# Mixture-of-experts dispatch on one core: the first expert's columns made first, 16-bit tables with the chunk innermost, a semaphore per first gathered tile

## What is computed

```python
probs = softmax(xn @ router_w.T + router_b)          # 4096 x 8
gates, idx = top_k(probs.T, cap)                     # cap = 4096/8 = 512 tokens for each expert
xe = xn[idx]
hmid = gelu(einsum('ech,efh->ecf', xe, fc1_w) + fc1_b)      # 256 -> 1024
ye = einsum('ecf,ehf->ech', hmid, fc2_w) + fc2_b            # 1024 -> 256
out = zeros.at[idx].add(ye * gates)
out = out / max(sum of the gates of a token, 1e-9)
```

## Time and profile before

| | |
|---|---|
| runs | 1294.95, 1296.77, 1298.42 us; median 1296.77 |
| the profiled execution's own time | 1302.38 us |
| its span | 1300.7 us |
| mean granted TensorE clock | 0.91 |
| busy share: PE, DVE, ACT, POOL | 88%, 80%, 59%, 31% |
| instructions: PE, DVE, ACT, POOL | 8470, 2233, 929, 397 |
| self-attention and cross-attention | about 0 to 1000 us |
| routing and dispatch, PE nearly idle | about 1000 to 1067 us |
| eight experts | about 1067 to 1300 us |

### The profile page before, as it was taken

How to read it: one execution, slowest core, us unless ns; L and a number is a source line. 1 busy time by engine, 2 the same in 40 slices (tenths; PEclk the granted TensorE clock), 3 DMA queues, 4 the chain that set the end, 5 groups by cost and what they waited for, 6 DMA issues and landing times. The chain is left out here.

```text
span 1300.7 us, 24570 instructions
## 1 busy us (share of the span) xinstructions
PE 1138.8 (88%) x8470; PEld 625.0 (48%) x8470; DVE 1046.4 (80%) x2233; ACT 763.1 (59%) x929; POOL 399.1 (31%) x397
## 2 busy tenths in 40 slices
PE   5888799999999999899999999988874049999994
PEld 3555443333333333333333333357763038889984
DVE  6988799899999999899999999427775975666651
ACT  2333127788787888688887878843453004556561
POOL 5777861212021211121121000022100032665663
PEclk9988769999999999899999999989785557999997
DMA  3567565542244413431343000045422021454432
GB/s 107 169 221 230 202 121 164 107 97 49 46 83 79 73 38 67 80 73 35 68 84 76 19 15 16 19 117 205 148 69 86 0 65 49 129 157 105 113 97 25
DMA packets 84103, 120.38 MB, mean 93 GB/s; under 512 B 23248, under 2 KB 57040, under 8 KB 82960
## 3 DMA queue, kind: packets, MB, share of 16 engines
q1 hardware_dynamic: 64832, 75.84, 18.9%
q0 software_dynamic: 15984, 39.86, 16.4%
q10 hardware_dynamic: 3168, 3.15, 0.8%
HBM read 75.67 MB, written 42.21 MB: 91 GB/s over the span
## 5 line engine op out<-in xcount | busy, mean ns | idle before, releaser
L696 DVE TENSOR_REDUCE b_max_halves<-banks 128x1 f32<-128x512 f32 x1024 | 628.8, 681 | 27.1 <-PE banks L763 26.8
L638 ACT ACTIVATE b_probs<-banks 128x1024 f32<-128x1024 f32 x512 | 519.9, 1025 | 143.0 <-PE banks L815 141.3
L763 PE MATMUL banks<-b_k,b_q 62*128 62x512 f32 x1024 | 400.5, 473 | 3.8 <-DVE b_max L713 2.1
L815 PE MATMUL banks<-b_q,b_k 64*128 64x512 f32 x1024 | 389.2, 458 | 11.5 <-DMA b_q<-b_max_rows 5.1
L785 PE MATMUL banks<-b_probs,b_v 128*32 128x256 f32 (+1 forms) x3840 | 321.9, 407 | 2.3 <-ACT b_out L625 0.3
L815 PEld LDWEIGHTS banks<-b_q,b_k 64*128 64x128 f32 x1024 | 161.1, 186 | 228.3 <-issue 154.4
L763 PEld LDWEIGHTS banks<-b_k,b_q 62*128 62x128 f32 x1024 | 166.5, 191 | 37.8 <-DVE b_max_halves L696 33.6
L785 PEld LDWEIGHTS banks<-b_probs,b_v 128*32 128x32 f32 x3840 | 76.0, 108 | 166.6 <-issue 86.8
L464 POOL TENSOR_TENSOR b_att<-b_out,b_rec_spread 128x512 f32<-128x512 f32 x32 | 41.1, 1284 | 309.0 <-DMA b_rec_spread<-reciprocals 308.8
L395 POOL DMA_DIRECT2D b_q<-q_stacks x60 | 31.7, 531 | 253.2 <-PE banks L785 233.4
L1693 DVE TENSOR_TENSOR e_hTl<-e_hT,e_hTh 128x512 fp32r<-128x512 f32 x64 | 44.5, 696 | 53.9 <-ACT e_hT L1453 53.9
(11 more groups left out here) (230 smaller groups left out, 1546.0 us busy)
## 6 DMA issues: line engine op xcount, KB each, us to landing
e_w<-in_w SPq DMA_DIRECT2D x16, 1024.0 KB
v_tiles<-a_v SPq DMA_DIRECT2D x8, 1024.0 KB, 9.1
q_stacks<-a_parts SPq DMA_DIRECT2D x32, 256.0 KB
k_stacks<-a_parts SPq DMA_DIRECT2D x32, 256.0 KB
b_q<-q_stacks POOLq DMA_DIRECT2D x30, 256.0 KB, 6.5
b_k<-k_stacks POOLq DMA_DIRECT2D x30, 256.0 KB, 7.2
b_v<-v_tiles POOLq DMA_DIRECT2D x15, 512.0 KB, 9.4
b_q<-b_max_rows SPq DMA_DIRECT2D x256, 2.0 KB
```

Of the source, the lines that this page charges most:

```text
L638: nc.scalar.activation(pr[:, S % NP, u], ps[:, 2 * u:2 * u + 2, :], ACT.Exp, scale=D ** -0.5).then_inc(s_ex[u], 1)
L696: v.tensor_reduce(mxp[:, (k // NB) % 2, s, p, t, kh:kh + 1], ps[:, bank(last), :], AX.X, ALU.max)\
L763: nc.tensor.matmul(ps[:, bank(last), :], qs[g][stack, p, at:at + P], ks[g][stack, p, CH * kh:CH * kh + CH], start=True, stop=True).then_in ...
L815: return nc.tensor.matmul(ps[:, 2 * u + s, :], ks[g][stack, u, P * kt:P * kt + P], qs[g][stack, u, CH * h:CH * h + CH], start=True, stop=True)
```

## The change

Six edits in `experts`:

1. **Layouts.** `hi`, `rv`, `w3` and `cmp_` have the chunk (or the block) innermost instead of the column. `tid`, the chunks' numbers, goes from 32 to 16 bits. The moving operand of a compaction now has its columns 32 elements of 16 bits apart.
2. **Two pieces.** The block tests and places are done for expert 0's 32 columns first (`first`), and for the 224 others (`others`) after expert 0's indicators.
3. **DVE's order.** `tokens(1)`, its indicators and `lower_w1` follow `first_slots(0)` in this order, the block tests of the others stand ahead of it; `rows(0)` stands ahead of `weights()`.
4. **Gathers of expert 0** count on a semaphore per tile, `s_g0[h]`; those of expert 2, 4 and 6 on `s_g[0]`, whose counts are 64 lower.
5. **Transposes.** `rows` on PE goes tile by tile (both halves of one tile, then the next), for every expert; for expert 0 it waits for each tile by itself.
6. **Expert 0's gate compaction** stands behind hidden unit 3 on PE, and so do `first_weights` and the tables of expert 2 on DVE.

```diff
-        hi = sb("d_hi", [P, 2, NTT, CT], BF16)
-        tid = sb("d_tid", [P, NTT])
+        hi = sb("d_hi", [P, 2, CT, NTT], BF16)
+        tid = sb("d_tid", [P, NTT], BF16)
-        w3 = sb("d_w3", [P, E * NTT, 3], BF16)
+        w3 = sb("d_w3", [P, 3, E * NTT], BF16)
-        rv = sb("d_rv", [P, 2, NTT, CT, NV], BF16)
+        rv = sb("d_rv", [P, 2, NV, CT, NTT], BF16)
-        cmp_ = sb("d_cmp", [P, 2, CT, NV])
+        cmp_ = sb("d_cmp", [P, 2, NV, CT])
+        s_g0 = [sem(f"e_first_tile{h}_gathered") for h in range(CT)]
...
                     g.indirect_dma_start(xe[:, x, h, :], None, xrow,
-                                         bass.IndirectOffsetOnAxis(ap=idx[:, n, h:h + 1], axis=0)).then_inc(s_g[x], 16)
+                                         bass.IndirectOffsetOnAxis(ap=idx[:, n, h:h + 1], axis=0))\
+                        .then_inc(s_g[x] if n else s_g0[h], 16)
...
-            for h in range(CT):
-                ins = v.tensor_scalar(ge[:, h, :], qf, P * h + 0.5, None, ALU.is_ge)
-            step(ins)
-            step(v.tensor_tensor(lo[:], ge[:, 1, :], ge[:, 2, :], ALU.add))
-            step(v.tensor_tensor(lo[:], lo[:], ge[:, 3, :], ALU.add))
-            step(v.scalar_tensor_tensor(lob[:], lo[:], -float(P), qf, ALU.mult, ALU.add))
+            def blocks(at):
+                for h in range(CT):
+                    ins = v.tensor_scalar(ge[:, h, at], qf[:, at], P * h + 0.5, None, ALU.is_ge)
+                step(ins)
+            def places(at):
+                step(v.tensor_tensor(lo[:, at], ge[:, 1, at], ge[:, 2, at], ALU.add))
+                step(v.tensor_tensor(lo[:, at], lo[:, at], ge[:, 3, at], ALU.add))
+                step(v.scalar_tensor_tensor(lob[:, at], lo[:, at], -float(P), qf[:, at], ALU.mult, ALU.add))
...
-                at = lambda h: ge[:, h:h + CT, chunks(n)].rearrange("p h k -> p k h")
+                at = lambda h: ge[:, h:h + CT, chunks(n)]
                 here(v.tensor_tensor(hi[:, x], at(0), at(1), ALU.subtract))
-                v.tensor_tensor(rv[:, x, :, :, 0], hi[:, x], tid[:].unsqueeze(2).to_broadcast([P, NTT, CT]), ALU.mult)
-                return v.tensor_scalar(rv[:, x, :, :, 1], hi[:, x], pid[:], None, ALU.mult)
+                v.tensor_tensor(rv[:, x, 0], hi[:, x], tid[:].unsqueeze(1).to_broadcast([P, CT, NTT]), ALU.mult)
+                return v.tensor_scalar(rv[:, x, 1], hi[:, x], pid[:], None, ALU.mult)
...
-            for n in range(2):
-                tokens(n, n)
-                if n == 1:
-                    first_slots(0)
-                    dve.wait_ge(s_w1h, 1)
-                    lower_w1()
-                for m in range(NTT // R):
-                    indicate(n, n, m)
+            first, others = slice(0, NTT), slice(NTT, E * NTT)
+            blocks(first)
+            places(first)
+            tokens(0, 0)
+            for m in range(NTT // R):
+                indicate(0, 0, m)
+            blocks(others)
+            first_slots(0)
+            places(others)
+            tokens(1, 1)
+            for m in range(NTT // R):
+                indicate(1, 1, m)
+            dve.wait_ge(s_w1h, 1)
+            lower_w1()
             first_slots(1)
+            rows(0)
             weights()
-            rows(0)
...
-                        if start and f == 1:
+                        if start and f == 3:
                             for m in range(2):
                                 first_weights(m)
...
-                    ins = mm(ps[:, 2, 0:CT * NV], oh[:, x, k // R, :, k % R], rv[:, x, k].rearrange("p h m -> p (h m)"),
+                    ins = mm(ps[:, 2, 0:CT * NV], oh[:, x, k // R, :, k % R], rv[:, x, :, :, k],
...
             def rows(i, x):
-                pe.wait_ge(s_g[x], 64 * i + 64)
-                for k in range(KC):
-                    for h in range(CT):
+                if not (isinstance(i, int) and i == 0 and x == 0):
+                    pe.wait_ge(s_g[x], 64 * i + (64 if x else 0))
+                for h in range(CT):
+                    if isinstance(i, int) and i == 0 and x == 0:
+                        pe.wait_ge(s_g0[h], 16)
+                    for k in range(KC):
...
-                        if start and f == 0:
+                        if start and f == 3:
                             pe.wait_ge(s_cc, 2)
                             pe.wait_ge(s_rvb, 1)
```

More of the change, by code:

```diff
@@ L1588, in tokens @@
                 here = Chain(dve, s_hi, n)
-                at = lambda h: ge[:, h:h + CT, chunks(n)].rearrange("p h k -> p k h")
+                at = lambda h: ge[:, h:h + CT, chunks(n)]
                 here(v.tensor_tensor(hi[:, x], at(0), at(1), ALU.subtract))
-                v.tensor_tensor(rv[:, x, :, :, 0], hi[:, x], tid[:].unsqueeze(2).to_broadcast([P, NTT, CT]), ALU.mult)
-                return v.tensor_scalar(rv[:, x, :, :, 1], hi[:, x], pid[:], None, ALU.mult)
+                v.tensor_tensor(rv[:, x, 0], hi[:, x], tid[:].unsqueeze(1).to_broadcast([P, CT, NTT]), ALU.mult)
+                return v.tensor_scalar(rv[:, x, 1], hi[:, x], pid[:], None, ALU.mult)
             def weigh(n, x):
-                return v.tensor_tensor(rv[:, x, :, :, 2:NV], hi[:, x].unsqueeze(3).to_broadcast([P, NTT, CT, 3]),
-                                       w3[:, chunks(n), :].unsqueeze(2).to_broadcast([P, NTT, CT, 3]), ALU.mult)
+                return v.tensor_tensor(rv[:, x, 2:NV], hi[:, x].unsqueeze(1).to_broadcast([P, 3, CT, NTT]),
+                                       w3[:, :, chunks(n)].unsqueeze(2).to_broadcast([P, 3, CT, NTT]), ALU.mult)
             def weights():
@@ L1610, in weights @@
                                      ALU.mult))
[L1611 to L1614, removed]
+                step(v.tensor_copy(w3[:, 0], wt[:]))
+                step(v.tensor_tensor(wr[:], wt[:], w3[:, 0], ALU.subtract))
+                step(v.tensor_copy(w3[:, 1], wr[:]))
+                step(v.tensor_tensor(w3[:, 2], wr[:], w3[:, 1], ALU.subtract))
                 for n in range(2):
@@ L1627, in first_slots @@
                 dve.wait_ge(s_cm, n + 1)
-                v.tensor_copy(cmp_[:, n, :, 0:2],
-                              ps[:, 2, 2 * P * n:2 * P * n + CT * NV].rearrange("p (h m) -> p h m", m=NV)[:, :, 0:2])\
+                v.tensor_copy(cmp_[:, n, 0:2],
+                              ps[:, 2, 2 * P * n:2 * P * n + 2 * CT].rearrange("p (m h) -> p m h", h=CT))\
                     .then_inc(s_cc, 1)
                 dve.wait_ge(s_cc, n + 1)
-                v.scalar_tensor_tensor(idx[:, n, :], cmp_[:, n, :, 0], float(P), cmp_[:, n, :, 1], ALU.mult, ALU.add)\
+                v.scalar_tensor_tensor(idx[:, n, :], cmp_[:, n, 0], float(P), cmp_[:, n, 1], ALU.mult, ALU.add)\
                     .then_inc(s_ix, 1)
@@ L1637, in first_weights @@
                 dve.wait_ge(s_cmb, 2)
-                v.tensor_copy(cmp_[:, n, :, 2:NV],
-                              ps[:, 2, 2 * P * n:2 * P * n + CT * NV].rearrange("p (h m) -> p h m", m=NV)[:, :, 2:NV])\
+                v.tensor_copy(cmp_[:, n, 2:NV],
+                              ps[:, 2, 2 * P * n + 2 * CT:2 * P * n + CT * NV].rearrange("p (m h) -> p m h", h=CT))\
                     .then_inc(s_ccb, 1)
                 dve.wait_ge(s_ccb, n + 1)
-                step(v.tensor_tensor(wx[:, n, :], cmp_[:, n, :, 2], cmp_[:, n, :, 3], ALU.add))
-                v.tensor_tensor(wx[:, n, :], wx[:, n, :], cmp_[:, n, :, 4], ALU.add).then_inc(s_wx, 1)
+                step(v.tensor_tensor(wx[:, n, :], cmp_[:, n, 2], cmp_[:, n, 3], ALU.add))
+                v.tensor_tensor(wx[:, n, :], wx[:, n, :], cmp_[:, n, 4], ALU.add).then_inc(s_wx, 1)
             def slots(n, x):
@@ L1648, in slots @@
                 dve.wait_ge(s_cm, n + 1)
-                v.tensor_copy(cmp_[:, x].rearrange("p h m -> p (h m)"), ps[:, 2, 0:CT * NV]).then_inc(s_cc, 1)
+                v.tensor_copy(cmp_[:, x].rearrange("p m h -> p (m h)"), ps[:, 2, 0:CT * NV]).then_inc(s_cc, 1)
                 dve.wait_ge(s_cc, n + 1)
                 loop = Chain(dve, s_dex, 2 * n - 4)
-                part = lambda m: cmp_[:, x:x + 1, :, m]
+                part = lambda m: cmp_[:, x:x + 1, m]
                 loop(v.scalar_tensor_tensor(idx[:, at, :], part(0), float(P), part(1), ALU.mult, ALU.add))
@@ L1765, in first_compact @@
             def first_compact(n, part, m, s):
-                o = ps[:, 2, 2 * P * n:2 * P * n + CT * NV].rearrange("p (h m) -> p h m", m=NV)
+                o = ps[:, 2, 2 * P * n:2 * P * n + CT * NV].rearrange("p (m h) -> p m h", h=CT)
                 for k in range(R * m, R * m + R):
-                    ins = mm(o[:, :, part], oh[:, n, k // R, :, k % R], rv[:, n, k, :, part], start=(k == 0), stop=(k == NTT - 1))
+                    ins = mm(o[:, part, :], oh[:, n, k // R, :, k % R], rv[:, n, part, :, k], start=(k == 0), stop=(k == NTT - 1))
                 if m == NTT // R - 1:
```

## The result

| | before | after |
|---|---|---|
| runs | 20, 1294.95 to 1311.0 us | 20, 1287.12 to 1303.87 us |
| median | 1302.15 us | 1294.82 us |
| profiled execution: span | 1300.7 us | 1298.8 us |
| block tests of expert 0 to the end (both profiles) | 253.84 us | 248.55 us |

The ratio of the times is 0.995, 95% interval 0.993 to 0.997: 3.9 to 9.1 us less, so faster by 0.3 to 0.7%, the lower end just at the 0.3% that the prediction called no change. Forecast: 1293.6 us in a range of 1290.0 to 1298.0, with "no change" the likeliest. The median lies 1.2 us from the number, but two errors cancelled there. The forecast started from 1296.77, the median of three runs; with twenty it is 1302.15. And the gain was put at 3.15 us; it is larger.

A forecast was written before the change was run, and what follows sets the result against it. TensorE bounds the kernel from 1100 us on, so the change works in the first expert's chain before it: -3.85 us to the first product, +0.7 for the weights' compaction, so 1296.77 - 3.15 = 1293.6 us, range 1290.0 to 1298.0.

The forecast's parts named there:

- Term 1: First expert's tables on VectorE, narrower and in order: slot numbers ready 1.7 us earlier.
- Term 2: First expert's four gather descriptor calls on GpSimd: 6.0 us instead of 6.8, 0.8 us gained.
- The collision: Fourth gather against SyncE's 1 MB load of expert 1's w1: call ends at 1058.5, ahead of 1059.9, so it passes.
- the rival's picture: Fourth gather comes behind the w1 load and waits for all of it: first gain gone, 1296.7 us; chance 0.2.
- the page's rule: DMA engines go round-robin between queues packet by packet; a late gather would lose only about its own length.
- Term 3: First expert's transposes on TensorE: six done before the fourth gather, two left behind it; 1.35 us gained.
- Term 4: Weights' compaction moves from behind unit 0 to behind unit 3 of the up product; clock falls, +0.7 us.
- rival (a): Clock stays up through the weights' compaction in the up product: 5.45 us less in all, 1291.3 us; chance 0.2.
- If it falls, they take 7.8 again: Up product behind the weights' compaction: if the clock falls, 24 products take 7.8 us; 19.6 in all, 0.7 more.
- The signs of being wrong: Wrong if first product is not 3 us earlier, eight late compaction products exceed 0.52 us, or TensorE waits for `weights`.
- What costs nothing: Later experts' tables about a microsecond shorter on VectorE: worth zero, at most 0.3 us; strided compaction columns: nothing.

The follow-up runs named there:

- Layouts alone: Kernel before with only the layouts changed: median 1300.83 us of 10 runs against 1301.46 of 23, ratio 0.999 (0.9962 to 1.0018).
- residual early: Changed kernel with the residual of w1 ahead of expert 1's indicators instead of behind them: 1297.24 us in one run.
- the experiment: Changed kernel with TensorE waiting for all four tiles of expert 0 ahead of its first transpose: 1294.59 us in one run.
- the two spread kernels: Changed kernel with expert 2's indicators spread over units 3 to 6: median 1291.26 us; the same plus expert 0's columns in halves: median 1290.81 us.

## Why the prediction was right and wrong

**Term 1 (-1.7): right.** 6.92 to 5.24 is 1.68. The indicators start at +1.72, not +1.54, and the rest of the way is 0.17 shorter. Layouts alone give 0.6 of it; the narrow first piece and the order the rest.

**Term 2 (-0.8): right in the profile it was made for, for half a reason.** The four calls took 5.98 us instead of 6.8, forecast 6.0. The total was luck: the rule that carried it (a call ends 0.83 after the VectorE instruction that ran when it began) gave calls of 1.3, 1.3, 0.95, 1.5 us, where 1.09, 1.01, 1.48, 1.49 came; and in four of eight later profiles with the same work on VectorE two of them took about 0.96, and all four together 4.9 us. A median over runs may hold more than 0.8; one profile per kernel can't say how much.

**The collision: right, and narrow.** The load went out at +12.06 for a forecast of +12.0, behind the fourth call as forecast. Moving it 2.4 us earlier brought exactly the rival's picture: queue still for the whole load, 1.7 us lost. In both traces the gathers' queue starts again while the load's last packets move; in the kernel before there are 29 packets of the gathers' beside 47 of the load's from 1060.4 to 1061 us. What the prediction made of the page's rule was wrong, though. The Trainium skill (DMA: Bandwidth & Descriptors, "Queues, rings and completion order") has a DMA engine drain a whole packet of some 9 to 17 descriptors, at most 64, from one queue before it turns to the next. The profile lists 272 entries for the load (residual early, 1056 to 1061 us); by an estimate from the page's figure, if they are descriptors and 16 engines share them evenly, that is 17 each, which can be one packet of the page, and the gather's turn comes only after the load. So the three entries of the gathers' queue against 241 of the load's in 2.9 us don't speak against the page, and whether a longer load would be interrupted no run here shows.

**Term 3 (-1.35): right.** 6.36 to 5.10 us from the fourth call's end to the first product, 1.25 by the experiment. First product 3.78 us earlier for 3.85.

**Term 4 (+0.7): the mechanism right, the size not.** The clock did fall, in the compaction or within a microsecond of its end, in each of the nine profiles with the compaction behind unit 1 or 3; rival (a) is out. But from the first up product to the last it stayed at 18.91. "If it falls, they take 7.8 again" was wrong: the products behind it ran at 0.43 apart for 3.2 us, not 5.3, before the clock rose. In other profiles that stretch lasted up to 6.0 us, and the whole from 18.3 to 19.6; the mean of the eight with the compaction behind unit 3 is 19.2. So the term is 0.0 in this profile, +0.3 in the mean and between -0.6 and +0.7 over all, against the one profile of before; the size that I took is at the edge.

**The signs of being wrong.** None of the three came: the first product is 3.78 us earlier, eight late compaction products take 0.52 us as before, and TensorE doesn't wait for `weights` with the compaction behind unit 3 (behind unit 0 it does, for 1.37 us). The step that did fail had no sign of its own.

**"What costs nothing": the step that failed.** The prediction saw 0.3 us of waiting for an indicator table and called it "once", at most 0.3. It had read one row, that of TensorE's products. By the weight loads, TensorE waited for the first indicator table of each of five experts. Once the small tables ahead of it were short, 26.16 us from expert to expert became 25.91 in four of them and 26.26 became 25.82 in the first: 1.4 us, more than term 2. The same row that was used as proof of a bound, 99.26 of 100 us, had 0.74 us missing, and they were priced at zero.

**The sum.** 3.78 at the first product, 0.0 in the up product, 0.24 between down product and expert 1 (the clock rose 4.6 us after the down product's start, before 5.2), 1.4 in the periods, and 0.1 given back behind the last expert's transposes: 5.3, which is the 5.29 of the trace. The runs' 3.9 to 9.1 us hold it. The gain forecast was 3.15, and that the median came within 1.2 us of the forecast is luck: the starting point was 5.4 too low and the gain, by the medians 7.3, was put 4.2 too low.

**The chances.** "No change" had 0.53 because the sum stood at 3.15 with a bound at 3.9; with 1.4 for the layouts and 0 for term 4 it would have stood at 5.25, beyond the bound. The base of three runs hid this in the number itself: 1302.15 - 3.15 would have been 1299.0, 4.2 above what was measured. The profiled execution's own 1302.38 was in sight and turned out nearer to the level of twenty runs.

## What to carry to other kernels

When an engine is nearly full, ask what fills the missing per cent, and read the rows of its weight loads as well as of its products: a wait of 0.3 us repeated in every round is worth more than a stage's single microsecond. Follow a chain from a mark in the program, not from the start of the span, when what lies ahead of it varies by more than the change is worth. And where a large transfer and a small late one share the DMA engines, keep the small one's issue ahead: here an order 2.4 us worse brought the first product 1.7 us later.

## What the runs showed of the hardware

- A gather call of the same form lasted 0.95 to 1.49 us in the changed kernel beside the same VectorE work, and differed between two profiles of the same program (0.97 and 1.48 for the third).
- Packets of an indexed gather whose call ended 1.4 us after a 1 MB load's issue did not move until the load was all but through: 3 packets of the gathers' queue against 241 in 2.9 us. With the call's end 0.4 us ahead of the issue they passed.
- In the kernel with the compaction behind unit 0, one packet of the `instruction` queue took 1.7 us of a DMA engine while a gather's packets moved: 45 of them came in time and three with the next gather's.
- Tables of 128 elements in 16 bits took 0.22 us with their inputs in order and 0.44 with the chunk strided; a moving operand of 20 columns, 64 bytes apart, made the compaction's products 218 ns instead of 211, while eight of them took 0.52 us in both.
- 4.0 to 4.1 us of small products (64 compaction products), with TensorE counted as busy throughout, were followed by a fall of the granted clock from 1.00 to 0.50, within them or 0.3 us behind them, in each of the eight profiles in which they began at 1.00. With 32 such products in 2.2 us, straight behind dense ones (the two spread kernels), it stayed at 1.00.
